# Two heads in one stack buffer, and the products of two passes issued side by side

## What is computed

```python
scores = jnp.einsum('bhqd,bhkd->bhqk', q, k) / math.sqrt(Hd)
pos = jnp.arange(S)
rel = jnp.abs(pos[None, :] - pos[:, None]).astype(jnp.float32)
bias = -slopes[:, None, None] * rel
probs = jax.nn.softmax(scores + bias[None], axis=-1)
out = jnp.einsum('bhqk,bhkd->bhqd', probs, v)
```

## Time and profile before

| What | us |
|---|---|
| median of 3 runs | 2316.67 |
| the runs | 2316.25, 2316.67, 2319.93 |
| span of the profiled execution | 2319.1 |
| PE busy in it | 1785.6 (77%) |
| VectorE busy | 1705.7 (74%) |
| ScalarE busy | 1040.3 (45%) |
| GpSimd busy | 952.0 (41%) |

### The profile page before, as it was taken

How to read it: one execution, slowest core, us unless ns; L and a number is a source line. 1 busy time by engine, 2 the same in 40 slices (tenths; PEclk the granted TensorE clock), 3 DMA queues, 4 the chain that set the end, 5 groups by cost and what they waited for, 6 DMA issues and landing times. The chain is left out here.

```text
span 2319.1 us, 57716 instructions
## 1 busy us (share of the span) xinstructions
PE 1785.6 (77%) x15650; PEld 1289.9 (56%) x15650; DVE 1705.7 (74%) x5837; ACT 1040.3 (45%) x1967; POOL 952.0 (41%) x1028
## 2 busy tenths in 40 slices
PE   2699999999999839999627777777777778389980
PEld 1466766666676639998514444444444444168860
DVE  3488888888888746676448989999998999434433
ACT  0266666666666612222115555555555556322220
POOL 0234444444344324444335455455455454223430
PEclk9999999999999969999858999999999999689995
DMA  3334444444444222222254444444544443111118
GB/s 122 49 70 72 74 75 73 70 75 76 72 74 75 52 69 70 68 66 65 64 127 85 94 83 86 95 82 82 94 86 80 96 85 70 51 52 47 54 38 253
DMA packets 273109, 183.80 MB, mean 79 GB/s; under 512 B 24461, under 2 KB 264973, under 8 KB 272206
## 3 DMA queue, kind: packets, MB, share of 16 engines
q1 hardware_dynamic: 251418, 151.21, 33.2%
q0 software_dynamic: 13312, 27.68, 4.4%
q10 hardware_dynamic: 8320, 4.19, 0.6%
HBM read 86.98 MB, written 48.96 MB: 59 GB/s over the span
## 5 line engine op out<-in xcount | busy, mean ns | idle before, releaser
L845 DVE TENSOR_REDUCE mx<-A 128x2 f32<-128x512 f32 x1024 | 692.9, 683 | 128.6 <-PE A L1087 52.3
L697 ACT ACTIVATE probs<-B 128x1024 f32<-128x1024 f32 x512 | 524.0, 1023 | 354.3 <-PE B L1110 184.2
L1083 PE MATMUL A<-stack 126*128 126x256 bf16 x2048 | 440.5, 287 | 162.2 <-DVE mx L845 129.4
L1107 PE MATMUL B<-stack 128*128 128x256 bf16 x2048 | 364.4, 281 | 32.1 <-DMA stack<-mrow 31.9
L1083 PEld LDWEIGHTS A<-stack 126*128 126x128 bf16 x2048 | 180.7, 100 | 332.0 <-DVE mx L845 246.6
L1307 POOL DMA_INDIRECT expert_out<-yt,row_dest x224 | 223.2, 996 | 335.9 <-DVE yt L1406 277.1
L1122 PE MATMUL M<-probs,vals 128*32 128x256 f32 x4096 | 289.7, 399 | 21.4 <-DVE On L871 17.2
L607 POOL DMA_INDIRECT gathered<-h,slot_in x192 | 187.1, 974 | 153.8 <-DVE slot_in L978 108.1
L1107 PEld LDWEIGHTS B<-stack 128*128 128x128 bf16 x2048 | 203.3, 103 | 83.7 <-issue 32.2
L1491 PE MATMUL A<-w2s,hid 128*128 128x128 f32 x1792 | 230.4, 278 | 11.2 <-issue 11.2
L596 POOL TENSOR_TENSOR h<-xn,back_rows 128x256 f32<-128x256 f32 x64 | 46.4, 724 | 466.6 <-DVE xn L799 466.6
(11 more groups left out here) (190 smaller groups left out, 3011.6 us busy)
## 6 DMA issues: line engine op xcount, KB each, us to landing
stack<-parts SPq DMA_DIRECT2D x768, 64.0 KB
xt<-gathered SPq DMA_DIRECT2D x112, 132.0 KB, 2.2
back_rows<-mod_rows SPq DMA_DIRECT2D x64, 192.0 KB, 3.2
w<-in_w SPq DMA_DIRECT2D x4, 2048.0 KB
x_mid<-X SPq DMA_DIRECT2D x64, 128.0 KB, 3.5
Y<-expert_out SPq DMA_DIRECT2D x64, 128.0 KB, 3.4
front_rows<-mod_rows SPq DMA_DIRECT2D x32, 192.0 KB, 3.3
X<-in_x SPq DMA_DIRECT2D x32, 128.0 KB, 3.1
```

What stands on the lines that cost most here:

```text
L697: act.activation(probs[c % 4][:, :, :, :], Bp[c % 2][:, :, :, :], ACT.Exp, scale=EXP_SCALE[l][c // 4]).then_inc(b_exp.handle, 1)
L845: dve.tensor_reduce(mx[u][:, h, :], A[h % 2][:, :, :], AX.X, ALU.max).then_inc(a_max.handle, 1)
L1083: ins = pe.matmul(A[h % 2][:, t, :], stack[u][0:n, h, 0, t * P:(t + 1) * P], stack[u][0:n, h, 1, :], start=True, stop=(l == 1))
L1107: ins = pe.matmul(Bp[c % 2][:, j, t, :], stack[u][:, h, 1, t * P:(t + 1) * P], stack[u][:, h, 0, :], start=True, stop=(l == 1))
```

## The change

A head now takes only half of the partitions. `MROW` moves from 126 to 50, right behind the 50 linear rows, so a head's rows are 0 to 51 (`ROWS`). Even heads of a pair stand at partitions 0 to 51, odd heads at 64 to 115 (`HALF`), and one buffer holds 8 pairs. There are four such buffers instead of two, chosen by the batch modulo 4, so the loop body holds four ticks. The total size of the stacks is unchanged. The zeroing of the stacks falls away.

The second argument of `stack_up` is no longer a half: it issues all 12 transfers of batch i+1 in tick i, the six of the even heads first, and waits for the second pass of four batches before instead of two. `stack_max` is two transfers instead of one, each of half the rows.

`scores` replaces `scores_a` and `scores_b`. For n from 0 to 15 it issues head n of the first pass of batch i next to head n+1 (n even) or n-1 (n odd) of the second pass of batch i-1: product A for one tile, product B for the same tile, which use different halves of the partitions, then the same for the other tile, then in layer 0 the distance products of both. Both waits, for the first pass and for the second, stand ahead of the pair. The second half of the maxima is turned after pair 1 instead of after head 6, and ScalarE's `max_rows` for it moves to right after its first exponential. Weights and constants are reordered to match.

```diff
-MROW = P - 2
+MROW = LIN + 2
+ROWS = MROW + 2
+HALF = P // 2
+STACKS = 4
...
-        stack = [sb(f"stack{u}", [P, H, 2, S], BF16) for u in range(2)]
+        stack = [sb(f"stack{v}", [P, HH, 2, S], BF16) for v in range(STACKS)]
...
-                for u in range(2):
-                    dve.memset(stack[u][:, :, :, :], 0.0).then_inc(stack_zero, 1)
...
+    def slot(i):
+        return lambda off: (i + off) % STACKS
...
-    with eng.Fori(0, pairs) as k:
+    with eng.Fori(0, rounds) as k:
...
-            def stack_up(b, k, u, half):
-                if half == 0:
-                    sp.wait_ge(split.handle, split.after(b))
-                sp.wait_ge(b_scores.handle, b_scores.after(b - 2, 4 * half + 4))
-                for r, (pq, pk) in enumerate(PRODUCTS):
-                    src = parts[u][:, :, :, :].rearrange("p q r s -> p (q r) s")
-                    sp.dma_start(stack[u][HD * r:HD * r + HD, HH * half:HH * half + HH, :, :],
-                                 src[64 * half:64 * half + 64, pq:4 + pk:3 + pk - pq, :])\
-                        .then_inc(stack_in[u][half], 16)
-
-            def stack_max(b, k, u, half):
+            def stack_up(b, k, u, v):
+                sp.wait_ge(split.handle, split.after(b))
+                if not isinstance(b, int) or b >= STACKS:
+                    sp.wait_ge(b_scores.handle, b_scores.after(b - STACKS, HH))
+                for j in range(2):
+                    for r, (pq, pk) in enumerate(PRODUCTS):
+                        src = parts[u][:, :, :, :].rearrange("p q r s -> p (q r) s")
+                        first = HALF * j + HD * r
+                        sp.dma_start(stack[v][first:first + HD, :, :, :],
+                                     src[HALF * j:HALF * j + HALF, pq:4 + pk:3 + pk - pq, :])\
+                            .then_inc(stack_in[u][j], 16)
+
+            def stack_max(b, k, u, v, half):
                 sp.wait_ge(mT_read.handle, mT_read.after(b, half + 1))
-                sp.dma_start(stack[u][MROW:MROW + 2, HH * half:HH * half + HH, 0, :], mrow[half][:, :])\
-                    .then_inc(m_in[u][half], 16)
+                for j in range(2):
+                    first = HALF * j + MROW
+                    sp.dma_start(stack[v][first:first + 2, 4 * half:4 * half + 4, 0, :], mrow[half][8 * j:8 * j + 8, :])\
+                        .then_inc(m_in[u][half], 16)
...
-            def tick(at):
-                if at(0):
-                    stack_up(*at(0), 1)
+            def tick(at, slot):
                 if at(-1):
-                    stack_max(*at(-1), 1)
+                    stack_max(*at(-1), slot(-1), 1)
...
                 if at(1):
-                    stack_up(*at(1), 0)
+                    stack_up(*at(1), slot(1))
...
                 chunk(0)
+                step(max_rows, -1, 1)
...
-                step(max_rows, -1, 1)
...
+            def scores(at, slot, n):
+
+                c, j = n // 2, n % 2
+                if at(0):
+                    b, k, u = at(0)
+                    if n < 2:
+                        pe.wait_ge(stack_in[u][j], stack_in.of(k))
+                    pe.wait_ge(a_max.handle, a_max.after(b, n - 1) if n >= 2 else a_max.after(b - 1, H + n - 1))
+                if at(-1) and j == 0:
+                    b, k, u = at(-1)
+                    if c % 4 == 0:
+                        pe.wait_ge(m_in[u][c // 4], m_in.of(k))
+                    pe.wait_ge(b_exp.handle, b_exp.after(b, c - 1) if c >= 2 else b_exp.after(b - 1, HH + c - 1))
                 for t in range(NT):
...
+                    if at(0):
+                        rows = stack[slot(0)][HALF * j:HALF * j + MROW, c, :, :]
+                        last_a = pe.matmul(A[j][:, t, :], rows[:, 0, t * P:(t + 1) * P], rows[:, 1, :],
+                                           start=(t == 0), stop=(l == 1), skip_group_check=True)
+                    if at(-1):
+                        rows = stack[slot(-1)][HALF * (1 - j):HALF * (1 - j) + ROWS, c, :, :]
+                        last_b = pe.matmul(Bp[c % 2][:, 1 - j, t, :], rows[:, 1, t * P:(t + 1) * P], rows[:, 0, :],
+                                           start=(t == 0), stop=(l == 1), skip_group_check=True)
+                if l == 0:
+                    for t in range(NT):
+                        if at(0):
+                            last_a = pe.matmul(A[j][:, t, t * P:(t + 1) * P], slope_ident[:, n % HH, :],
+                                               dist[:, t, :], start=False, stop=True, skip_group_check=True)
+                    for t in range(NT):
+                        if at(-1):
+                            last_b = pe.matmul(Bp[c % 2][:, 1 - j, t, t * P:(t + 1) * P], slope_ident[:, (n + 1 - 2 * j) % HH, :],
+                                               dist[:, 1 - t, :], start=False, stop=True, skip_group_check=True)
+                if at(0):
+                    last_a.then_inc(a_scores.handle, 1)
+                if at(-1) and j == 1:
+                    last_b.then_inc(b_scores.handle, 1)
...
-                a_pass(0, 1)
-                chunk(0)
-                a_pass(2)
+                pair(0)
+                pair(1)
+                if at(-1):
+                    m0_read((h_ready, 1), (mT_read, -1, 1))
+                    turn_max(*at(-1), 1)
+                pair(2)
                 heads_step(weigh, -2, 3)
...
-                a_pass(3)
-                chunk(1)
+                pair(3)
                 if at(1):
-                    m0_read((h2T_read, -3))
+                    m0_read((h2T_read, -3), (mT_read, -1, 2))
                     project_qk(*at(1))
...
-                a_pass(15)
+                pair(15)
                 if at(0):
                     m0_read((pos_read, -3), *[(x1_ready, -2)] * (l == 0), (v_ready, 0))
                     turn_max(*at(0), 0)
-                chunk(7)
```

More of the change, by code:

```diff
@@ L261, in build @@
         ]
-        stack_rows = [(stack[u][first:first + 2, :, :, :], a["stack_rows0"][n:n + 2].bitcast(BF16))
-                      for u in range(2) for n, first in ((0, LIN), (2, MROW))]
+        stack_rows = [(stack[v][HALF * j + LIN:HALF * j + ROWS, :, :, :], a["stack_rows0"][j].bitcast(BF16))
+                      for v in range(STACKS) for j in range(2)]
         loaded, ready, modp, moded, mod_out = (sem(n) for n in
             ("setup_loaded", "setup_ready", "setup_products", "setup_modulation", "mod_rows_written"))
-        stack_zero, stack_loaded = sem("setup_stack_zeroed"), sem("setup_stack_loaded")
+        stack_loaded = sem("setup_stack_loaded")
         set_act, set_dve = sem("setup_act_order"), sem("setup_dve_order")
@@ L372, in peeled @@
         return lambda off: (i + off, (i + off) // 2, (i + off) % 2) if 0 <= i + off < B else None
+    def slot(i):
+        return lambda off: (i + off) % STACKS
     for i in range(-DEPTH, DEPTH):
-        tick(peeled(i))
-    pairs = (B - 2 * DEPTH) // 2
+        tick(peeled(i), slot(i))
+    rounds = (B - 2 * DEPTH) // STACKS
     if ch:
         ch.before()
-    with eng.Fori(0, pairs) as k:
+    with eng.Fori(0, rounds) as k:
         if ch:
-            ch.loop(k, 2 * per)
-        for i in (DEPTH, DEPTH + 1):
-            tick(lambda off: (k * 2 + (i + off), k + (i + off) // 2, (i + off) % 2))
+            ch.loop(k, STACKS * per)
+        for i in range(DEPTH, DEPTH + STACKS):
+            tick(lambda off: (k * STACKS + (i + off), k * (STACKS // 2) + (i + off) // 2, (i + off) % 2), slot(i))
         if ch:
-            assert ch.n == 2 * per, ch.n
+            assert ch.n == STACKS * per, ch.n
     if ch:
-        ch.done(pairs)
-    for i in range(DEPTH + 2 * pairs, B + DEPTH):
-        tick(peeled(i))
+        ch.done(rounds)
+    for i in range(DEPTH + STACKS * rounds, B + DEPTH):
+        tick(peeled(i), slot(i))
 def attention(nc, l, g):
@@ L427, in attention @@
     stack_in = Transfers([[sem(f"stack_in{u}{h}") for h in range(2)] for u in range(2)], len(PRODUCTS))
-    m_in = Transfers([[sem(f"m_in{u}{h}") for h in range(2)] for u in range(2)], 1)
+    m_in = Transfers([[sem(f"m_in{u}{h}") for h in range(2)] for u in range(2)], 2)
     x1_out = transfers("x1_out", 1)
@@ L850, in split_max @@
                 dve.wait_ge(m_T.handle, m_T.after(b - 1, half + 1))
-                v = mx[u][:, HH * half:HH * half + HH, :].rearrange("p h t -> p t h")
-                ch.link(dve.tensor_scalar(mneg[:, half, :, 0, :], v, -1.0, None, ALU.mult))
-                dve.scalar_tensor_tensor(out=mneg[:, half, :, 1, :], in0=v, scalar=-1.0, in1=mneg[:, half, :, 0, :],
+                v = mx[u][:, half, :, :, :].rearrange("p t j i -> p (t j) i")
+                hi, lo = (mneg[:, half, :, :, n, :].rearrange("p t j i -> p (t j) i") for n in range(2))
+                ch.link(dve.tensor_scalar(hi, v, -1.0, None, ALU.mult))
+                dve.scalar_tensor_tensor(out=lo, in0=v, scalar=-1.0, in1=hi,
```

(9 more changed lines are left out.)

99 lines of the change are left out of this document (34 added, 65 removed).

## The result

The changed kernel takes 2705 us (median of 4, 2703.6 to 2707.8) where the kernel before takes 2317: 1.167 times as long, interval 1.166 to 1.169. The forecast was 2593 us, range 2460 to 2700, slower 0.91. The direction held, and the loop that the forecast described is there, but it is one of two. The size did not hold: 389 us were added and 276 forecast, and the time lies 5 us above the range.

What follows compares the result with a forecast made beforehand. VectorE was busy most of each attention tick, and a faster PE could give only 1.2 us; a new transfer loop would set ticks. 31 x (5.4 + 3.5) = 276 us on 2319.1 gives 2595, less 0.1% 2593; range 2460 to 2700.

Steps and rivals of the forecast that it cites:

- What bounds the kernel, and what a faster PE can give: Steady attention ticks, 22.6 and 25.0 us: VectorE's waits for PE are 1.2 us a tick, all a faster PE can give.
- none of this is on the new loop except pair(0) to pair(3): PE's gains from pairing, 0.6 us a tick in layer 0 and 2.1 in layer 1, lie mostly off the loop.
- The loop that this closes: From pair(0) through q/k read, split, twelve stack transfers and mrow transfers to the next pair(0): 27.5 and 28.0 us.
- Layer 0: 28.0 us a tick: Layer 0's steady tick: 6.7 + 4.8 + 15.2 + 0.8 = 27.5, plus 0.5 for the clock; 5.4 above 22.6.
- Layer 1: 28.5 us a tick: Layer 1's steady tick: loop of 28.5, 28.0 with an earlier split, plus 0.5 for the clock; 3.5 above 25.0.
- A loop body of four ticks saves a branch now and then: Loop of either layer: a four-tick body was to save under 0.3 us in four ticks.
- 31 steps of a layer with the steady difference: Both layers, batch to batch: 31 x (5.4 + 3.5) = 276 us added.
- The clock: PE after idling at a tick's end, pair(0) to project_qk: lower clock costs 0.5 us a tick, bounds 0 and 1.9.
- or the clock stays low: Rival, also covering products not side by side: pair(0) to pair(3) grow up to 2 us a tick, 2686 us; chance 0.10.
- Eight engines and two: DMA side: a stack transfer uses eight engines, an mrow transfer two of these; the trace's 4.0 us was said to agree.
- loads at SP's pace: Rival: twelve stack transfers land in 10.0 us and the mrow wait decides; 2319 to 2393 us, middle 2350; chance 0.09.
- Faster: Rival: the array pairs well, nothing new waits, VectorE never waits for PE; 2245 us; chance 0.05.

Runs made afterwards that it cites:

- experiment 10: Changed kernel with product B on the same half of the partitions as product A, so nothing runs side by side: 2940 us, ratio 1.272.
- experiment 5: Changed kernel with the first half of the maxima turned after pair(12) instead of pair(15), run again beside the changed kernel: 2687 us, ratio 1.158.
- experiment 2: Changed kernel with six of a batch's twelve stack transfers cut to one head pair from batch 4 on: 2618 us, ratio 1.127.
- experiment 4: Changed kernel with the projection of q and k and its read moved to the start of the tick: 2558 us, ratio 1.104.
- experiment 6: Changed kernel with all 38 ticks of a layer written out, no loop: 2682 us, ratio 1.157.
- experiment 1: Kernel before, with only the loop body changed from two ticks to four: 2371 us, ratio 1.023.
- the best version tried: Changed kernel written out, with early q/k projection, early turn of the maxima's first half, and GpSimd's scatter wait moved behind the next split: 2492 us, ratio 1.073.
- the one with the early turn 2694: Changed kernel with the first half of the maxima turned after pair(12), first run, in the group where the kernel before took 2449 us: 2694 us.

## Why the forecast was right, and where it was not

*What bounds the kernel, and what a faster PE can give*: pairing works and brings nothing against the kernel before; PE idles 3 to 5 us a tick. But "none of this is on the new loop except pair(0) to pair(3)" was wrong: without it the changed kernel takes 233 us more (experiment 10). PE's whole tick up to the last turn lies on the second loop.

*The loop that this closes*: right as a mechanism (experiment 5: with the other loop opened the tick stays), incomplete as an account. A second loop of about the same length runs through the tick's own products to the last turn (experiment 2). The forecast had the mrow pair late because of its place in SP's queue; SP is in fact idle when it comes. In layer 0 both loops end at 27.4 us. Opening either alone brought 16 us (the second) and 87 (most of the first's transfers); the 147 us of experiment 4 came from shortening both.

*Layer 0: 28.0 us a tick*: 27.9 measured, by luck: errors that cancel. Reading q and k came at 8.3 us, not 7.2 (6.7 + 0.5 for the clock), the twelve transfers took 14.1, not 15.2, mrow landed with them instead of 0.8 later, and pair(0) started 0.5 after that.

*Layer 1: 28.5 us a tick*: this is the step that failed; 31.4 measured. Its terms, forecast and measured: q and k read 6.2 and 7.7; wait and split 4.9 and 5.0; from the first stack issue to the last landing 15.2 and 16.4; to mrow's landing 2.2 and 2.1; pair(0) after it 0 and 0.2. The sum misses 2.9 us, 90 us in 31 ticks and so most of the 112 that were not forecast; the late q and k and the slow transfers are 2.7 of it. Nearly half, 1.4 us a tick, goes when the loop is written out (experiment 6, where q and k are read at 6.9 us).

*"A loop body of four ticks saves a branch now and then"*: wrong, the term with the wrong sign. It costs the kernel before 53 us (experiment 1). The changed kernel written out takes 21 us less (experiment 6), 2682 us, inside the range; VectorE stops there 4 to 7 us at each branch back, part of it while PE waits anyway. The count of VectorE's instructions per body stood in the trace.

*31 steps of a layer with the steady difference*: held. From the first maximum of the first batch to that of the last, layer 0 grew by 176 us (forecast 167) and layer 1 by 202 (forecast 109); 31 times the steady difference as measured, 6.4 us, is 198. The first tick of layer 1 grew most, from 18.5 to 36.2 us, but the others a little less than 6.4. Some 10 us more lie between and behind the two stretches. The forecast missed 9 + 93 + 10 = 112 us, and of the 93 the steady tick is 90.

*The clock*: 0.5 us may have been low: q and k, which depend on the order and the clock, came 1.1 us later than forecast in layer 0. In layer 1 the clock is at the lower of its two levels (1.2 instead of 2.4 GHz) more often than not: the mean is 0.69, where PE waits 4.6 us a tick for mrow. What the clock costs by itself no run shows, so whether the bounds 0 and 1.9 us held stays open too, and so does how much of the rival "or the clock stays low" came true in layer 1.

*Pairing*: forecast 3 us of PE in layer 0 if it failed; experiment 10 measures 3.8 us a tick over both layers. The rival "not side by side", priced at 2686, would have been 2940.

*Eight engines and two*: the 4.0 us of the earlier trace rows show only that an mrow transfer waits behind others. The landings show more: in the trace of the changed kernel the semaphores move nine times for each stack transfer (1728 for 192) and three times for each mrow transfer (192 for 64), one step and eight or two more.

*Rivals*: loads at SP's pace fell (27.4 against 23.3 for the last landing; even with small transfers 2618 us). "Faster" fell: the time is 1.167 times that before, and 1.073 in the best version tried, in which layer 1 still waits for loads and for mrow.

## What to carry to other kernels

When a wait is put ahead of a pipeline's first instruction, write down every chain that ends there, not only the one that was changed: here two were about equally long, and what counted was to shorten both. Before a loop body is doubled, count each engine's instructions in it: VectorE's went from 305 to 540 and more and it stopped 3 to 7 us at each branch back, and writing the ticks out was faster than either loop (by 0.8% and by 3%). A small transfer that the start of a tick needs lands late behind a backlog of others; here neither an earlier issue nor ScalarE's queue brought it home in time.

## What was not expected of the hardware

From VectorE's branch back to its next instruction are 0.3 us with 305 instructions in the body, 3.2 us with 540 or 601, and 6.6 us in layer 1 of the changed kernel. Written out, the same work shows no such stop (2301 us).

In one group of runs, on another chip, the kernel before took 2449 us (2443 to 2456) instead of 2317 to 2321 us, while the changed kernel flat took 2682 us there and elsewhere, and the one with the early turn 2694 and 2687. Versions between were 1 to 2% slower there (2580 and 2547, 2558 and 2510). No trace of the kernel before on that chip exists; the cause stays open.
